# State-space layer: two decoder products of each batch computed in the next batch's turn, and the second norm's affine placed ahead of the first norm's sums and logarithms

## The chip, the cores and the metric

The kernel runs on one core of a Trainium2 chip. The metric is the device time of one execution in microseconds (us); the median of the runs is compared. The core has a matrix engine (TensorE, PE in the profile), a vector engine (VectorE, DVE), a scalar engine (ScalarE, ACT), GpSimd (POOL) and SyncE (SP), which here only issues DMAs. Each engine works through its own list of instructions in order and waits on semaphores.

## The reference

The program is a stack of four layers on an input of 8 batches x 384 channels x 1024 tokens, each layer added to its input after a group norm: attention, a state-space layer, depthwise convolutions, and an RWKV layer. The change touches the second one alone. Its reference, cut (x enters group-normalised; LN is a layer norm over the 384 channels with gain and bias):

```python
fx  = LN(u, ln1_g, ln1_b)                      # the first norm
Bu  = einsum('ph,blh->blp', B_bar, fx)         # complex
xs  = scan over tokens of  lam_bar * x + Bu
y   = gelu(2 * real(einsum('hp,blp->blh', Cc, xs)) + D * fx) + fx
fy  = LN(y, ln2_g, ln2_b)                      # the second norm
z1, z2 = split(fy @ W_enc.T, 2)
y   = (z1 * gelu(z2)) @ W_dec.T + fy
x   = x + y
```

## The kernel before

The layer is `s5_layer`. The channels lie on 128 partitions x 3 tiles (CT = 3), the 1024 tokens are worked in two halves of 512 columns. Everything is float32; one matmul of the program is two passes of the array, so that the trace counts twice as many as the code.

The engines' lists are unrolled over the batches in **turns**. In turn i three batches are in flight: batch i ("here") has its second norm, the encoder, the gates and the decoder; batch i+1 ("after") has the B products, the scan and the C products; batch i+2 ("third") has its group norm and its first norm. Turns -3 to -1 fill this pipeline. Turns 0 to 5 hold all three, turn 6 has no third batch, turn 7 only "here". Names of the steps, with the lines of the kernel before:

- `fill_b` (L1462): 8 products of batch i+1 into PSUM, four per half; `turn_in` (L1288 to L1302) on DVE reads them. `sums` (L831) averages over channels for both norms, on tiles that DVE (`add_tiles`, L1358) or POOL (L1149 to L1157, first norm) have added up. The first norm's squares (`squares`, ACT, L842) and POOL's sums lie in the tile `hid`, which later in the turn holds the gated hidden state.
- `inverses` (ACT, L846 and L849) makes 1/sqrt of the variances by a logarithm and an exponential, first for the second norm of batch i and then for the first norm of batch i+2. `scale` (DVE, L853) multiplies by it, and `affine` (ACT, L1190) applies gain and bias. `f_made` tells PE that `y` is normalised.
- `fill_enc` (L1474): 12 products of batch i, two for each (tile, half), 36 matmuls. ACT makes a gelu of the one (`gates`, L1198) and DVE multiplies it by the other into `hid` (`apply_gate`, L1331).
- `fill_dec` (L1485): 6 products from `hid`, 18 matmuls. DVE adds the normalised `y` to the reloaded input `xres` (`add_residual`, L1336), adds the products (L1344) and measures the result (L1348 to L1354), all in `outputs`.
- `scan` (L1306) and `turn_out` (L1325) on DVE, then `fill_c` (L1495), 24 matmuls, and `activations` (L1372 to L1377).

The products share a ring of 4 PSUM banks. The list `ORDER` gives every product its place, its bank is place % 4, and `wait_for_bank` makes PE wait for the reader of the product four places earlier. SP loads `xin` (the input of batch i+3, for the group norm), stores `xres` when all six outputs of a batch are made, and then reloads it with the next batch.

Of the kernel before, what the change touches and what calls it, by code (L numbers as in the profile page):

```python
# [855 lines left out]
def s5_layer(nc, const, x_in, x_out, moments_out, w):  # L856
# [12 lines left out]
    with ExitStack() as ctx:  # L869
# [19 lines left out]
        hid = sb("hid1", [P, CT, T])  # L889
        u = sb("u1", [P, TILES, T])  # L890
# [208 lines left out]

        ORDER = []  # L1100
        for i in range(-1, B):
            if i + 1 < B:
                ORDER += [("b", i + 1, n) for n in range(2 * TILES)]
            if i >= 0:
                ORDER += [("enc", i, n) for n in range(4 * CT)] + [("dec", i, n) for n in range(2 * CT)]
            if i + 1 < B:
                ORDER += [("c", i + 1, n) for n in range(2 * CT)]
# [15 lines left out]
        def _(sp):  # L1123
            for i in range(-3, B):
# [5 lines left out]
                if i >= 0:  # L1130
                    sp.wait_ge(out_made.sem, out_made.at(2 * CT, i))
                    sp.dma_start(x_out[i:i + 1].rearrange("a (p t) n -> p (a t n)", t=CT), xres[:, :, :].rearrange("p t n -> p (t n)")).then_inc(stored, 16)
                    if i + 1 < B:
                        sp.wait_ge(out_measured.sem, out_measured.at(1, i))
                        sp.wait_ge(stored, 16 * (i + 1))
                        sp.dma_start(xres[:, :, :].rearrange("p t n -> p (t n)"), x_in[i + 1:i + 2].rearrange("a (p t) n -> p (a t n)", t=CT)).then_inc(res_loaded, 16)
# [3 lines left out]
        def _(pool):  # L1140

            for i in range(-2, B):
                if batch(i + 2):
                    f = f1[i % 2]
                    for half in range(2):
                        at = hid[:, 0, cols(half)]
# [5 lines left out]
                    for half in range(2):  # L1152
                        at = hid[:, 0, cols(half)]
                        pool.wait_ge(squared1.sem, squared1.at(half + 1, i + 2))
                        pool.tensor_tensor(at, at, hid[:, 1, cols(half)], ALU.add).then_inc(summed_sq1.next(), 1)
                        pool.wait_ge(summed_sq1.sem, summed_sq1.at(2 * half + 1, i + 2))
                        pool.tensor_tensor(at, at, hid[:, 2, cols(half)], ALU.add).then_inc(summed_sq1.next(), 1)  # L1157

        @block.scalar
        def _(act):  # L1160
# [39 lines left out]
            for i in range(-2, B):  # L1200
# [6 lines left out]
                if batch(i + 2):  # L1207
                    squares(norm1, hid, f1[i % 2], centred1, squared1, i + 2)
                if batch(i):
                    inverses(norm2, varied2, inv_made2, i)  # L1210
                if batch(i + 2):
                    inverses(norm1, varied1, inv_made1, i + 2)
                if batch(i):
                    affine(y, rows["ln2_g"], rows["ln2_b"], scaled2, f_made, i)
# [16 lines left out]
        def _(dve):  # L1231
# [106 lines left out]
            def outputs(i):  # L1338
                for n in range(2 * CT + 1):
                    if n < 2 * CT:  # L1340
# [1128 lines left out]
```

## Time and profile before

| | us |
|---|---|
| median of 3 runs | 4383.45 (4381.31 to 4385.81) |
| the profiled execution: its time | 4377.48 |
| its span | 4375.8 |
| PE busy in the span | 3968.0 (91%) |
| DVE busy | 3072.4 (70%) |
| ACT busy | 2265.1 (52%) |
| POOL busy | 1373.9 (31%) |

The state-space layer takes from about 1852 to 2779 us of the span. The shares of busy time are averages over four different layers, and say nothing on this one; what bounds it is read from the list of instructions in order of time (the timeline) of its turns, where the brackets give the idle time of the engine before an instruction and what ended it. Turn 2 runs from 2202 to 2305 us. "us" behind a start is the sum of the durations of the merged instructions; the end of a matmul is modelled. Starts are the better ruler.

### The profile page before, as it was taken

To read this page: it belongs to the slowest core of one execution; us is meant where nothing else is said; L and a number is where in the kernel's file an instruction comes from. 1 tells how busy PE (TensorE), PEld (TensorE's weight loads), DVE (VectorE), ACT (ScalarE), POOL (GpSimd) and SP (SyncE) were. 2 spreads that over 40 slices of the span, in tenths; PEclk is the share of its full clock that TensorE was granted. 3 is DMA by queue.
4 is the path that set the end of the run, shared out by engine and by line. 5 is a ranking of instruction groups with operands and counts; after the bars stand their busy time and mean duration, and the time that the engine had idled before them with its cause. 6 is when DMAs were issued, how large, how long until landed. Compare 5 with 4: busy or idle time off the path is not lost. (4 is left out here: it accounts for less than half of the span.)

```text
span 4375.8 us, 53839 instructions
## 1 busy us (share of the span) xinstructions
PE 3968.0 (91%) x17283; PEld 2342.1 (54%) x17283; DVE 3072.4 (70%) x3124; ACT 2265.1 (52%) x3601; POOL 1373.9 (31%) x1108
## 2 busy tenths in 40 slices
PE   6999999999999999849999998565899999999999
PEld 5777777777767686424444443244344444444444
DVE  4757575767676765476777766444879879878878
ACT  2858586767677777643333332222445544544544
POOL 2858575757576666521111110222000000000000
PEclk8999999999999999969999999788899999999999
DMA  4323232333333332120111100567110110110110
GB/s 134 87 81 106 75 104 80 100 90 96 93 91 99 86 104 68 57 75 15 58 58 44 44 29 29 145 177 227 47 43 0 43 43 0 43 43 0 43 43 14
DMA packets 114250, 307.91 MB, mean 70 GB/s; under 512 B 47634, under 2 KB 49250, under 8 KB 104306
## 3 DMA queue, kind: packets, MB, share of 16 engines
q1 hardware_dynamic: 105522, 272.56, 20.3%
q0 software_dynamic: 7504, 24.80, 2.2%
q10 hardware_dynamic: 1008, 7.67, 0.5%
q8 instruction: 136, 2.23, 0.2%
q14 instruction: 80, 0.66, 0.1%
HBM read 203.12 MB, written 101.30 MB: 70 GB/s over the span
## 5 line engine op out<-in xcount | busy, mean ns | idle before, releaser
L417 POOL TENSOR_TENSOR probs_lo<-probs,probs_hi 128x512 fp32r<-128x512 f32 x848 | 1170.6, 1396 | 633.2 <-ACT probs L463 612.6
L530 DVE TENSOR_REDUCE maxima<-m_psum 128x1 fp32r<-128x1024 f32 x512 | 625.1, 1222 | 364.9 <-PE m_psum L706 364.0
L462 ACT ACTIVATE probs_hi<-s_psum 128x512 fp32r<-128x512 f32 x1024 | 613.2, 599 | 380.2 <-PE o_psum L735 218.6
L2390 PE MATMUL psum<-mixes,last_weights 128*128 128x512 f32 x1728 | 751.1, 592 | 0.0
L463 ACT ACTIVATE probs<-s_psum 128x512 f32<-128x512 f32 x1024 | 609.0, 595 | 0.0
L2390 PEld LDWEIGHTS psum<-mixes,last_weights 128*128 128x128 f32 x1728 | 327.5, 190 | 409.8 <-issue 409.8
L719 PE MATMUL s_psum<-q_all,k_hi 128*128 128x512 f32 x1024 | 429.7, 420 | 25.4 <-ACT probs L463 25.1
L735 PE MATMUL o_psum<-probs_lo,v 128*112 128x512 f32 x1024 | 411.4, 402 | 13.6 <-DVE probs_lo L610 6.5
L720 PE MATMUL s_psum<-q_all,k_lo 128*128 128x512 f32 x1024 | 403.0, 394 | 0.0
L730 PE MATMUL o_psum<-probs_hi,v 128*112 128x512 f32 x1024 | 402.7, 393 | 0.0
L2397 PE MATMUL psum<-xp,last_weights 128*128 128x512 f32 x864 | 383.2, 597 | 18.3 <-DVEq L2274 13.3
L706 PE MATMUL m_psum<-k_hi,q_all 128*128 128x512 f32 x1024 | 342.2, 416 | 31.5 <-DVE maxima L530 18.2
L706 PEld LDWEIGHTS m_psum<-k_hi,q_all 128*128 128x128 f32 x1024 | 289.2, 324 | 73.9 <-DVE maxima L530 26.5
L1474 PE MATMUL psum<-y,enc_w 128*128 128x512 f32 x576 | 263.6, 620 | 30.3 <-ACT y L1190 30.3
L2397 PEld LDWEIGHTS psum<-xp,last_weights 128*128 128x128 f32 x864 | 162.2, 189 | 233.4 <-issue 208.4
L719 PEld LDWEIGHTS s_psum<-q_all,k_hi 128*128 128x128 f32 x1024 | 194.7, 190 | 120.9 <-ACT probs L463 97.3
L1865 PE MATMUL psum<-xt,last_weights 32*32 32x240 f32 (+3 forms) x5376 | 136.6, 453 | 112.5 <-issue 80.1
L735 PEld LDWEIGHTS o_psum<-probs_lo,v 128*112 128x112 f32 x1024 | 178.7, 175 | 89.8 <-POOL probs_lo L417 22.3
L1474 PEld LDWEIGHTS psum<-y,enc_w 128*128 128x128 f32 x576 | 114.2, 200 | 180.3 <-issue 141.7
L610 DVE TENSOR_TENSOR probs_lo<-probs,probs_hi 128x512 fp32r<-128x512 f32 x176 | 193.1, 1097 | 20.1 <-ACT probs L463 18.9
L720 PEld LDWEIGHTS s_psum<-q_all,k_lo 128*128 128x128 f32 x1024 | 193.4, 189 | 25.6
L730 PEld LDWEIGHTS o_psum<-probs_hi,v 128*112 128x112 f32 x1024 | 178.9, 175 | 45.6
(327 smaller groups left out, 6018.8 us busy)
## 6 DMA issues: line engine op xcount, KB each, us to landing
xin<-x SPq DMA_DIRECT2D x17, 1536.0 KB, 6.8
xin<-in_x SPq DMA_DIRECT2D x16, 1536.0 KB, 7.4
k_hi<-k_rows_hi SPq DMA_DIRECT2D x128, 192.0 KB, 3.4
xres<-x SPq DMA_DIRECT2D x16, 1536.0 KB, 7.0
k_rows_hi<-stage_hi SPq DMA_DIRECT2D x48, 256.0 KB, 2.1
k_rows_lo<-stage_lo SPq DMA_DIRECT2D x48, 256.0 KB, 2.3
q_rows_hi<-stage_hi SPq DMA_DIRECT2D x48, 256.0 KB, 2.5
q_rows_lo<-stage_lo SPq DMA_DIRECT2D x48, 256.0 KB, 2.6
```

Source lines behind the costliest of these rows:

```text
L417: pool.tensor_tensor(probs_lo[:, u % RING, :], probs[:, u % RING, :], as_f32(probs_hi[:, u % RING, :]), ALU.subtract).then_inc(pool_low.ne ...
L462: nc.scalar.activation(probs_hi[:, u % RING, :], s_psum[:, u % 2, :], ACT.Exp, scale=SCALE)
L463: nc.scalar.activation(probs[:, u % RING, :], s_psum[:, u % 2, :], ACT.Exp, scale=SCALE).then_inc(exped.next(), 1)
L530: nc.vector.tensor_reduce(maxima[:, g % 2, tile:tile + 1], source, AX.X, ALU.max, negate=True).then_inc(rows_max.next(), 1)
L706: ins = nc.tensor.matmul(pair_of(other)[:, half, :], q_all[:, g % SLOTS, tile::KEYS], k_hi[:, g % SLOTS, cols_of(half)], start=True, stop= ...
L719: nc.tensor.matmul(s_psum[:, u % 2, :], k_hi[:, h % SLOTS, keys], q, start=True, stop=False)
L720: nc.tensor.matmul(s_psum[:, u % 2, :], k_lo[:, h % SLOTS, keys], q, start=False, stop=True).then_inc(scored.next(), 1)
L730: nc.tensor.matmul(o_psum[0:USED, half, :], v[:, tile, h, :], probs_hi[:, u % RING, :], start=(tile == 0), stop=False)
L735: nc.tensor.matmul(o_psum[0:USED, half, :], v[:, tile, h, :], probs_lo[:, u % RING, :], start=False, stop=(tile == KEYS - 1)).then_inc(wei ...
L1474: ins = nc.tensor.matmul(bank("enc", i, 2 * n + k), enc_w[:, t, first + m * P:first + (m + 1) * P], y[:, t, cols(half)], start=(t == 0), s ...
L2390: ins = nc.tensor.matmul(bank, conv_w[:, t, down, factor, m * P:(m + 1) * P], mixes[:, factor, t, down:down + S, :].rearrange("p a b -> p ...
L2397: ins = nc.tensor.matmul(bank.rearrange("p (a b) -> p a b", b=S), weights[:, t, m * P:(m + 1) * P], rows_of(t, half), start=(t == 0), stop ...
```

## The change

It does five things.

1. `fill_dec` and `outputs` take a range. Of a batch's six decoder products, n = 0 to 3 are computed in its own turn and n = 4 and 5 in the next one, by PE behind `fill_b` and ahead of the first norm's second `sums`; DVE adds and measures them behind `turn_in`. The last batch computes all six in its own turn. `ORDER` follows.
2. POOL's sums and ACT's squares of the first norm move from `hid` into a tile of their own, `first_sums`, since `hid` now holds data of the batch before at that time.
3. On ACT, `affine` of the second norm stands ahead of `inverses` of the first norm.
4. On DVE, `scale` of the first norm moves behind `moments` and the first `scan`, and two scans stand behind it.
5. SP stores batch i-1 and reloads `xres` for batch i in turn i instead of at the end of turn i-1.

```diff
+        first_sums = sb("first_sums", [P, CT, T])
...
+        EARLY = 4
+        def early(i):
+            return EARLY if i + 1 < B else 2 * CT
         for i in range(-1, B):
             if i + 1 < B:
                 ORDER += [("b", i + 1, n) for n in range(2 * TILES)]
+            if i >= 1:
+                ORDER += [("dec", i - 1, n) for n in range(EARLY, 2 * CT)]
             if i >= 0:
-                ORDER += [("enc", i, n) for n in range(4 * CT)] + [("dec", i, n) for n in range(2 * CT)]
+                ORDER += [("enc", i, n) for n in range(4 * CT)] + [("dec", i, n) for n in range(early(i))]
@@ block.sync, behind the load of xin
-                if i >= 0:
-                    sp.wait_ge(out_made.sem, out_made.at(2 * CT, i))
-                    sp.dma_start(x_out[i:i + 1].rearrange("a (p t) n -> p (a t n)", t=CT), xres[:, :, :].rearrange("p t n -> p (t n)")).then_inc(stored, 16)
-                    if i + 1 < B:
-                        sp.wait_ge(out_measured.sem, out_measured.at(1, i))
-                        sp.wait_ge(stored, 16 * (i + 1))
-                        sp.dma_start(xres[:, :, :].rearrange("p t n -> p (t n)"), x_in[i + 1:i + 2].rearrange("a (p t) n -> p (a t n)", t=CT)).then_inc(res_loaded, 16)
+                if i >= 1:
+                    store(i - 1)
+                    sp.wait_ge(out_measured.sem, out_measured.at(1, i - 1))
+                    sp.wait_ge(stored, 16 * i)
+                    sp.dma_start(xres[:, :, :].rearrange("p t n -> p (t n)"), x_in[i:i + 1].rearrange("a (p t) n -> p (a t n)", t=CT)).then_inc(res_loaded, 16)
+            store(B - 1)
@@ block.scalar
                 if batch(i):
                     inverses(norm2, varied2, inv_made2, i)
+                    affine(y, rows["ln2_g"], rows["ln2_b"], scaled2, f_made, i)
                 if batch(i + 2):
                     inverses(norm1, varied1, inv_made1, i + 2)
                 if batch(i):
-                    affine(y, rows["ln2_g"], rows["ln2_b"], scaled2, f_made, i)
                     gates(i, 0, 2)
@@ block.vector
-                if third:
-                    scale(norm1, f1[i % 2], inv_made1, scaled1, i + 2)
+                if batch(i - 1):
+                    outputs(i - 1, EARLY, 2 * CT)
                 if batch(i + 3):
                     moments(i + 3)
                 if after:
                     scan(i + 1, 0)
-                    scan(i + 1, 1)
+                if third:
+                    scale(norm1, f1[i % 2], inv_made1, scaled1, i + 2)
                 if here:
                     apply_gate(i, 0)
                 if after:
+                    scan(i + 1, 1)
                     scan(i + 1, 2)
...
-                    outputs(i)
+                    outputs(i, 0, early(i))
@@ block.tensor
                 if after:
                     fill_b(i + 1, 1, 2, TILES)
+                if batch(i - 1):
+                    fill_dec(i - 1, EARLY, 2 * CT)
                 if third:
-                    sums(norm1, norm_psums[0], hid[:, 0, :], summed_sq1, varied1, i + 2)
+                    sums(norm1, norm_psums[0], first_sums[:, 0, :], summed_sq1, varied1, i + 2)
                 if here:
                     fill_enc(i)
-                    fill_dec(i)
+                    fill_dec(i, 0, early(i))
```

PE in turn 2, before (matmuls as the code counts them; f_1 is the normalised batch i+1, `norm_1` belongs to the second norm, `norm_0` to the first):

```order
L1462 MATMUL psum<-f_1,b_w 128x512 x6
L831 MATMUL norm_1<-z,col_mean 128x512 x2
L1462 MATMUL psum<-f_1,b_w 128x512 x9
L831 MATMUL norm_0<-hid,col_mean 128x512 x2
L1462 MATMUL psum<-f_1,b_w 128x512 x3
L831 MATMUL norm_1<-z,col_mean 128x512 x2
L1462 MATMUL psum<-f_1,b_w 128x512 x6
L831 MATMUL norm_0<-hid,col_mean 128x512 x2
L1474 MATMUL psum<-y,enc_w 128x512 x36
L1485 MATMUL psum<-hid,dec_w 128x512 x18
L1495 MATMUL psum<-u,c_w 128x512 x24
```

and now, where L1479, L1491, L1502 and L1512 are the new lines of the b, enc, dec and c products:

```order
L1479 MATMUL psum<-f_1,b_w 128x512 x6
L831 MATMUL norm_1<-z,col_mean 128x512 x2
L1479 MATMUL psum<-f_1,b_w 128x512 x9
L831 MATMUL norm_0<-first_sums,col_mean 128x512 x2
L1479 MATMUL psum<-f_1,b_w 128x512 x3
L831 MATMUL norm_1<-z,col_mean 128x512 x2
L1479 MATMUL psum<-f_1,b_w 128x512 x6
L1502 MATMUL psum<-hid,dec_w 128x512 x6
L831 MATMUL norm_0<-first_sums,col_mean 128x512 x2
L1491 MATMUL psum<-y,enc_w 128x512 x36
L1502 MATMUL psum<-hid,dec_w 128x512 x12
L1512 MATMUL psum<-u,c_w 128x512 x24
```

Six matmuls on `hid` (the two products put off by turn 1) stand between the last b products and the first norm's sums of squares, and twelve instead of eighteen stand behind the encoder.

DVE in turn 2 from the end of `turn_in` to the first two gates, before:

```order
L1302 TENSOR_TENSOR u<-u,prod 128x512
L853 TENSOR_TENSOR f_0<-f_0,ln_inv 128x3x512 x2
L104 BN_STATS gn_stats<-xin 128x6 x6
L115 BN_AGGR gn_both<-gn_stats 128x2
L118 SCALAR_TENSOR_TENSOR gn_both<-gn_both 128x1
L1306 SCALAR_TENSOR_TENSOR z<-decay,u 128x1024 x2
L1331 TENSOR_TENSOR hid<-gate,psum 128x512
L1306 SCALAR_TENSOR_TENSOR z<-decay,u 128x1024
L1331 TENSOR_TENSOR hid<-gate,psum 128x512
```

and now, where L1315 is the end of `turn_in`, L1357 to L1369 are `outputs`, L1319 is the scan and L1344 the gate:

```order
L1315 TENSOR_TENSOR u<-u,prod 128x512
L1357 TENSOR_TENSOR xres<-xres,psum 128x512 x2
L1361 BN_STATS out_stats<-xres 128x6 x2
L1367 BN_AGGR x_moments<-out_stats 128x2
L1369 SCALAR_TENSOR_TENSOR x_moments<-x_moments 128x1
L104 BN_STATS gn_stats<-xin 128x6 x6
L115 BN_AGGR gn_both<-gn_stats 128x2
L118 SCALAR_TENSOR_TENSOR gn_both<-gn_both 128x1
L1319 SCALAR_TENSOR_TENSOR z<-decay,u 128x1024
L853 TENSOR_TENSOR f_0<-f_0,ln_inv 128x3x512 x2
L1344 TENSOR_TENSOR hid<-gate,psum 128x512
L1319 SCALAR_TENSOR_TENSOR z<-decay,u 128x1024 x2
```

Six instructions of `outputs` (two sums, two measurements, two small ones) stand ahead of the moments, and the first gate has one scan less and these six more in front of it.

ACT in turn 2, from the logarithms of the second norm (`norm_1`) to the gates, before:

```order
L846 ACTIVATE ln_inv<-norm_1,eps 128x512 x2
L849 ACTIVATE ln_inv<-ln_inv 128x512 x2
L846 ACTIVATE ln_inv<-norm_0,eps 128x512 x2
L849 ACTIVATE ln_inv<-ln_inv 128x512 x2
L1190 ACTIVATE y<-y,ln_b_c,ln_g_c 128x512 x6
L1198 ACT_TABLE_LOAD
L1198 ACTIVATE gate<-psum 128x512 x2
```

and now:

```order
L846 ACTIVATE ln_inv<-norm_1,eps 128x512 x2
L849 ACTIVATE ln_inv<-ln_inv 128x512 x2
L1202 ACTIVATE y<-y,ln_b_c,ln_g_c 128x512 x6
L846 ACTIVATE ln_inv<-norm_0,eps 128x512 x2
L849 ACTIVATE ln_inv<-ln_inv 128x512 x2
L1210 ACT_TABLE_LOAD
L1210 ACTIVATE gate<-psum 128x512 x2
```

The six affine instructions on `y` moved ahead of the four instructions of the first norm's (`norm_0`) logarithms and exponentials.

## Rows read from the trace of the kernel before

**Rows 1.** Timeline of PE in turn 2: start, us, engine, line, instruction, count, idle before.

```profile
2202.36 5.40 PE L1462 MATMUL psum<-f,b_w 128*128 128x512 f32 x12
...
2228.42 1.02 PE L831 MATMUL norm<-hid,col_mean 128*128 128x512 f32 x2
2231.05 1.12 PE L831 MATMUL norm<-hid,col_mean 128*128 128x512 f32 x2 [1.61 <-POOL hid L1157]
2236.25 32.87 PE L1474 MATMUL psum<-y,enc_w 128*128 128x512 f32 x72 [4.08 <-ACT y L1190]
2268.96 15.61 PE L1485 MATMUL psum<-hid,dec_w 128*128 128x512 f32 x36
2284.41 20.76 PE L1495 MATMUL psum<-u,c_w 128*128 128x512 f32 x48
...
2305.15 5.40 PE L1462 MATMUL psum<-f,b_w 128*128 128x512 f32 x12
```

**Rows 2.** Timeline of PE in other turns, from turn 0 to turn 7.

```profile
1995.26 5.40 PE L1462 MATMUL psum<-f,b_w 128*128 128x512 f32 x12
...
2544.15 34.22 PE L1474 MATMUL psum<-y,enc_w 128*128 128x512 f32 x72 [4.08 <-ACT y L1190]
...
2614.26 5.31 PE L1462 MATMUL psum<-f,b_w 128*128 128x512 f32 x12
...
2639.02 31.17 PE L1474 MATMUL psum<-y,enc_w 128*128 128x512 f32 x72 [0.34 <-ACT y L1190]
...
2724.47 32.81 PE L1474 MATMUL psum<-y,enc_w 128*128 128x512 f32 x72 [5.49 <-ACT y L1190]
```

**Rows 3.** Stretches: length, busy of each engine, granted TensorE clock, DMA share, GB/s.

```profile
2236.00:2242.00 6.00, 5.75 (x10) 2.54 (x11) 5.92 (x8) 4.19 (x6) 0.00 (x0) 0.69 0.00 0
2614.00:2706.00 92.00, 91.66 (x213) 40.13 (x213) 62.42 (x75) 19.77 (x26) 0.00 (x0) 1.00 0.09 35
```

**Rows 4.** Timeline of ACT in turn 2.

```profile
2232.93 1.15 ACT L849 ACTIVATE ln_inv<-ln_inv 128x512 f32<-128x512 f32 x2
2233.99 4.33 ACT L1190 ACTIVATE y<-y,ln_b_c,ln_g_c 128x512 f32<-128x512 f32 x6
```

**Rows 5.** Timeline of DVE in turn 2, from the second norm's scale to the fourth gate.

```profile
2227.39 5.22 DVE L853 TENSOR_TENSOR y<-y,ln_inv 128x1536 f32<-128x1536 f32 x2 [0.26 <-ACT ln_inv L849]
...
2234.94 3.41 DVE L853 TENSOR_TENSOR f<-f,ln_inv 128x1536 f32<-128x1536 f32 x2
2238.27 3.64 DVE L104 BATCH_NORM_STATS2 gn_stats<-xin 128x6 f32<-128x512 f32 x6
...
2242.55 4.47 DVE L1306 TENSOR_TENSOR_SCAN z<-decay,u 128x1024 f32<-128x1024 f32 x2
...
2254.83 0.68 DVE L1331 TENSOR_TENSOR hid<-gate,psum 128x512 f32<-128x512 f32 x1
...
2259.98 0.68 DVE L1331 TENSOR_TENSOR hid<-gate,psum 128x512 f32<-128x512 f32 x1
```

**Rows 6.** Timeline of DVE in turn 2, end of the outputs.

```profile
2284.68 0.69 DVE L1344 TENSOR_TENSOR xres<-xres,psum 128x512 f32<-128x512 f32 x1 [1.28 <-PE psum L1485]
...
2287.06 0.22 DVE L1354 SCALAR_TENSOR_TENSOR x_moments<-x_moments 128x1 f32<-128x1 f32 x1
```

**Rows 7.** DMA issues of turn 2: count, KB each, median us from issue to landing.

```profile
x<-xres SPq DMA_DIRECT2D x1, 1536.0 KB, 5.0
xres<-x SPq DMA_DIRECT2D x1, 1536.0 KB, 6.2
```

**Rows 8.** Timeline of PE in turn -1, while the pipeline fills.

```profile
1935.73 1.88 PE L831 MATMUL norm<-hid,col_mean 128*128 128x512 f32 x4
```

**Rows 9.** Timeline of POOL in turn -1.

```profile
1932.83 1.27 POOL L1151 TENSOR_TENSOR hid<-hid,f 128x512 f32<-128x512 f32 x1
```

**Rows 10.** Timeline of DVE in turns -2 and -1.

```profile
1915.05 3.65 DVE L104 BATCH_NORM_STATS2 gn_stats<-xin 128x6 f32<-128x512 f32 x6
...
1948.47 3.43 DVE L853 TENSOR_TENSOR f<-f,ln_inv 128x1536 f32<-128x1536 f32 x2 [0.61 <-ACT ln_inv L849]
```

More of the change, by code:

```diff
@@ L1123, in _, with store @@
         def _(sp):
+            def store(i):
+                sp.wait_ge(out_made.sem, out_made.at(2 * CT, i))
+                sp.dma_start(x_out[i:i + 1].rearrange("a (p t) n -> p (a t n)", t=CT), xres[:, :, :].rearrange("p t n -> p (t n)")).then_inc(stored, 16)
             for i in range(-3, B):
@@ L1145, in _ @@
                     for half in range(2):
-                        at = hid[:, 0, cols(half)]
+                        at = first_sums[:, 0, cols(half)]
                         if half == 0:
@@ L1152, in _ @@
                     for half in range(2):
-                        at = hid[:, 0, cols(half)]
+                        at = first_sums[:, 0, cols(half)]
                         pool.wait_ge(squared1.sem, squared1.at(half + 1, i + 2))
-                        pool.tensor_tensor(at, at, hid[:, 1, cols(half)], ALU.add).then_inc(summed_sq1.next(), 1)
+                        pool.tensor_tensor(at, at, first_sums[:, 1, cols(half)], ALU.add).then_inc(summed_sq1.next(), 1)
                         pool.wait_ge(summed_sq1.sem, summed_sq1.at(2 * half + 1, i + 2))
-                        pool.tensor_tensor(at, at, hid[:, 2, cols(half)], ALU.add).then_inc(summed_sq1.next(), 1)
+                        pool.tensor_tensor(at, at, first_sums[:, 2, cols(half)], ALU.add).then_inc(summed_sq1.next(), 1)
         @block.scalar
@@ L1207, in _ @@
                 if batch(i + 2):
-                    squares(norm1, hid, f1[i % 2], centred1, squared1, i + 2)
+                    squares(norm1, first_sums, f1[i % 2], centred1, squared1, i + 2)
                 if batch(i):
                     inverses(norm2, varied2, inv_made2, i)
+                    affine(y, rows["ln2_g"], rows["ln2_b"], scaled2, f_made, i)
                 if batch(i + 2):
@@ L1336, in add_residual, with outputs @@
                 nc.vector.tensor_tensor(xres[:, :, cols(half)], xres[:, :, cols(half)], y[:, :, cols(half)], ALU.add).then_inc(res_added.next(), 1)
-            def outputs(i):
-                for n in range(2 * CT + 1):
-                    if n < 2 * CT:
+            def outputs(i, first, end):
+                for n in range(first, end + 1):
+                    if n < end:
                         m, half = n % CT, n // CT
@@ L1344, in outputs @@
                         nc.vector.tensor_tensor(xres[:, m, cols(half)], xres[:, m, cols(half)], bank("dec", i, n), ALU.add).then_inc(out_made.next(), 1)
-                    if n > 0:
+                    if n > first:
                         last = n - 1
@@ L1348, in outputs @@
                         nc.vector.bn_stats(out_stats[:, last, :], xres[:, last % CT, cols(last // CT)]).then_inc(step.next(), 1)
+                if end < 2 * CT:
+                    return
                 out = moments_out[:, i, :]
@@ L1476, in fill_enc, with fill_dec @@
                         ins.then_inc(hidden.next(), 1)
-            def fill_dec(i):
-                for n in range(2 * CT):
+            def fill_dec(i, first, end):
+                for n in range(first, end):
                     m, half = n % CT, n // CT
-                    if m == 0:
+                    if m == 0 or n == first:
                         pe.wait_ge(hid_made.sem, hid_made.at(CT * (half + 1), i))
@@ L1515, in _ @@
                 if third:
-                    sums(norm1, norm_psums[0], hid[:, 0, :], summed_x1, averaged1, i + 2)
+                    sums(norm1, norm_psums[0], first_sums[:, 0, :], summed_x1, averaged1, i + 2)
                 if after:
```

## The prediction, written before the changed kernel was run

> **What bounds the kernel now.** I read the timeline of each engine over one turn of the state-space layer, PE first. Turn 2 takes 102.79 us from its first b product to the next turn's [rows 1]. In it PE does 220 passes of the array. The 48 c passes take 20.6 us from start to start, 0.43 us each, and the 36 dec passes 15.45 us, the same [rows 1]; so PE's work is 94.4 us, and it waits or runs slowly for the other 8.4. All of that lies at one place. PE sits idle 1.61 us for POOL's sums of squares, then 4.08 us for ACT's affine of `y` [rows 1]. The 72 encoder passes that follow take 32.71 us from start to start, and 31.0 in turn 6 (31.17 less the 0.16 by which a duration there exceeds the distance of starts) [rows 1, 2]. The difference is the clock: 0.69 of 2.4 GHz was granted just behind the waits, that is, part of the stretch ran at 1.2 GHz, while all of turn 6, where PE idles 0.34 us, had 1.00 [rows 2, 3]. It costs 1.7 us in turn 2 and 3.05 in turn 5 [rows 1, 2]. The other 0.4 us are spread. So PE bounds every turn, but for one hole of some 8 us.
>
> The affine of `y` begins at 2233.99 with no idle before it, behind the exponentials of the first norm (2232.93), which in turn waited for POOL and PE [rows 4]. Its own input was ready much earlier: DVE scales `y` from 2227.39 on, two instructions in 5.22 us, so the first half is there by 2230.9 at the latest (5.22 less one unhindered 1.71) [rows 5]. The second norm thus waits for the first for no reason of data.
>
> **The new front of a turn (turns 1 to 5).** I keep turn 2's clock times. Up to 2228.42 PE has the same list [rows 1]. Then come 12 passes of the two put-off products (12 x 0.43 = 5.15), which cover POOL's end at about 2231, and 4 passes of sums (1.72): the encoder can start at 2235.3, 32.9 us into the turn, if what it waits for is there.
> - Affine: first half of `y` at 2230.9, three instructions of 0.72 (4.33 / 6) [rows 4]: 2233.0. In time. Before, this came at 2236.25.
> - Banks: the two products take banks whose readers are `turn_in`'s first four instructions of the second half, done before 2227.39 [rows 5]. The first encoder product takes that of the third b product, read right behind the scale of `y` (2232.6 + 0.6 = 2233.2). In time. The third and fourth encoder products wait for the put-off outputs on DVE, made by 2236.2, needed from 2240.5. In time.
> - The first norm is pushed back: sums by 2235.3, logarithms and exponentials (4 ACT instructions, 2.5 us) by 2238, the first gelu about 2239. DVE wants that norm's inverse only at 2244.6 (below).
>
> **The gates on DVE.** This is where the new order costs something. `turn_in` ends at 2234.94 [rows 5]. Then stand the outputs: one sum, two measurements and two small ones take 2.6 us (2284.68 to 2287.28) [rows 6], another sum 0.6: 3.2. Moments 4.28 (2238.27 to 2242.55), one scan 2.2 (4.47 / 2), the first norm's scale 3.33 (2234.94 to 2238.27) [rows 5]: 2248.0, and the first gate is done about 2248.65. PE's sixth encoder product needs it, five products of 2.58 behind 2235.3, at 2248.2. So PE waits about 0.45 us. From below it could be 0; from above, the outputs now cost as much as in their old place, where they come at PE's pace of 2.57 each, 5.1, and the wait is 2.4. I take 0.45, since both products are finished (2233.6) before DVE asks. Further gates lose nothing: DVE's step from gate to gate is 5.15 (2254.83 to 2259.98) [rows 5], and PE's pair of products takes 5.16. There is no cover left, though: here DVE and PE run neck and neck.
>
> **The turn sums.** Encoder 31.0 at full clock, four dec products 15.45 x 4 / 6 = 10.3, c products 20.6, group matmul 0.15.
> - Turns 1 to 4: 32.9 + 31.0 + 0.45 + 10.3 + 20.6 + 0.15 = 95.4 each, 381.6.
> - Turn 5 has no moments ahead of its gates and no group matmul behind: 94.8.
> - Turn 0 has nothing put off to it. The encoder starts with the affine at 2233.0, 30.6 into the turn: 92.7. It keeps 2.4 us of idle time; if the clock falls for it, up to 3 more.
>
> Together 569.1. Before, these six turns took 2614.26 - 1995.26 = 619.0 [rows 2]. **Gain 49.9.**
> - Turn 6 has the same number of products; its 0.34 us wait [rows 2] goes: gain 0.3.
> - Turn 7 has two products more. They stand where PE idles 5.49 us before the encoder [rows 2]: 5.15 us at full clock, 10.3 at half. The encoder's 32.81 there holds 1.6 of slow clock [rows 2], which busy PE may get back. Between a gain of 1.6 and a loss of 3.2; I take a gain of 1.0, because PE already runs its last sums just before.
> - Start: in turn -2 the moments (4.28) now stand ahead of the first norm's scale [rows 10]. That delay goes through ACT to POOL, whose sums for batch 1 end at 1938.4 and not 1934.1 [rows 9]. PE wants the second half at 1936.6 [rows 8]: 1.8 late. DVE's 0.61 us wait before the scale of turn -1 [rows 10] goes, as the moments fill it. A loss of 1.2; bounds 0 and 4.3.
>
> Sum: 49.9 + 0.3 + 1.0 - 1.2 = 50.0. The profiled execution's 4377.48 becomes 4327.5; it lay 6 us under the median, whose turns are the same, so I take the gain off the median: 4383.45 - 50.0 = **4333**.
>
> What lies beside: the DMAs. SP issues the store at 2236.2 instead of behind the outputs of the turn before, and the reload behind it: 5.0 and 6.2 us to land [rows 7], so `xres` is there at 2247.5. DVE adds it behind the fourth gate, about 2263.7. POOL's list is the same; its own tile removes no wait that showed.
>
> **Rivals.**
> - *DVE becomes the bound at the gates.* By the upper bound above, 2 us more in each of turns 1 to 4, 8 in all: 4341. For it: no slack. Against it: all six instructions have their inputs.
> - *The slow clock stays.* Turns 0 to 5 lose 1.7 to 3.05 us each as before [rows 1, 2], about 2.2 on average, 13 in all, though the idle time is down to some 0.5 us: 4346. Against it: turn 6 ran at 1.00 throughout with 0.34 us idle [rows 3]. The Trainium skill, "TensorE: Matmul & The Clock Gate", section "A second HAM failure mode: psum-queue depth-cycling", says that short idles between groups of matmuls that cycle through PSUM banks can be enough to make the clock swing; this kernel has such a ring of four banks, and by that rule this rival would hold, at its 4346. The trace disagrees in turn 6.
> - *The change does not do what it says:* the put-off products cannot start until `turn_in` is through (2234.94), because the ring holds them. Then the encoder starts at 2241.8, and turns 1 to 5 take 101.5 plus the slow clock, as before; only turn 0's 11 us are left: 4372. Against it: the banks' readers are done by 2227.39.
> - *The reload of `xres` comes late.* It is now inside the turn that needs it. It decides from about 2267, where the fifth gate, queued behind the add on DVE, holds a bank that PE wants; each us later costs one in 7 turns. To end 0.2% slower it must land 28 us after the 2247.5 of the rows, and gives 4392 there. Against it: 11.2 us for both transfers [rows 7] and a DMA queue with nothing else in it.
>
> **How the numbers follow.** The forecast 0.75, with a range of its own of 4326 (no wait at the gates, no loss at the start, the clock back in turn 7) to 4339 (turn 0's clock, a wait of 1 us, the loss in turn 7). DVE at the gates 0.10, slow clock 0.06, the ring 0.03, the late reload 0.06, of which half ends within 0.2%. The range 4325 to 4346 takes in the first three. A measurement of this kernel can tell about 0.2% from no change: faster by more 0.94, within it 0.03, slower 0.03.
>
> **What would show it.** Right: turns 1 to 4 at 95 to 96 us from first b product to first b product; no idle over 1 us before the encoder; clock 1.00 in turns 1 to 6; the encoder at 31.0 to 31.5; L853 on `f` behind a scan; PE waiting at most once a turn, in the encoder, for `hid` by DVE. Wrong: an idle of 2 us or more inside the encoder (DVE), encoder stretches above 32.5 with no idle inside (clock), an idle before the put-off products (ring), or DVE idle before L1349 for a DMA (reload). Turn 0's first b product more than 3 us later than 1995.26 [rows 2] would show that the start was mis-sized.

## The result, and the profile after

| | before | after |
|---|---|---|
| median | 4382.38 us (4379.58 to 4385.81, 4 runs) | 4331.14 us (4326.31 to 4335.67, 4 runs) |
| ratio, 95% interval | | 0.9883 (0.9865 to 0.99) |
| span of the profiled execution | 4375.8 us | 4329.4 us |
| PE busy in the span | 3968.0 us | 3959.5 us |

The kernel is 51.2 us faster; 50.0 had been forecast, and a time of 4333. To compare the layer alone, I measure from one event that both kernels have: the end of DVE's last instruction that builds the scan's tables, at 1911.7 us of the span before and 1917.5 after. From there to the first matmul of the next layer it is 867.7 us before and 817.1 after, 50.6 less. The profiled after entered the layer 5.8 us later, through the attention layer ahead of it, which the change does not touch; that is why the two profiled executions lie only 46 us apart.

First the timeline of PE in turn 2 after: start, summed duration, engine, line, instruction, count, idle before and what ended it. It answers to [rows 1].

```profile
2190.27 5.40 PE L1479 MATMUL psum<-f,b_w 128*128 128x512 f32 x12
...
2216.32 5.31 PE L1502 MATMUL psum<-hid,dec_w 128*128 128x512 f32 x12
2221.47 1.88 PE L831 MATMUL norm<-first_sums,col_mean 128*128 128x512 f32 x4
2223.19 13.04 PE L1491 MATMUL psum<-y,enc_w 128*128 128x512 f32 x30
2236.53 18.29 PE L1491 MATMUL psum<-y,enc_w 128*128 128x512 f32 x42 [0.30 <-DVE hid L1344]
2254.65 10.46 PE L1502 MATMUL psum<-hid,dec_w 128*128 128x512 f32 x24
2264.95 20.76 PE L1512 MATMUL psum<-u,c_w 128*128 128x512 f32 x48
...
2285.69 5.40 PE L1479 MATMUL psum<-f,b_w 128*128 128x512 f32 x12
```

Both waits of [rows 1], 1.61 us for POOL and 4.08 us for ACT, are gone. Twelve passes of the put-off products stand in their place, and one new wait of 0.30 us appears, for DVE's first gate. The turn takes 95.42 us instead of 102.79.

The stretches of PE's clock come next, with the columns of [rows 3]: turns 1 to 5 as a whole, turn 6, the front of turn 7, and its encoder.

```profile
2094.00:2571.00 477.00, 475.88 (x1113) 209.57 (x1112) 374.14 (x448) 165.29 (x215) 61.52 (x40) 1.00 0.12 47
...
2571.00:2662.00 91.00, 91.00 (x212) 40.02 (x212) 62.40 (x75) 19.77 (x26) 0.00 (x0) 1.00 0.09 35
2662.00:2681.00 19.00, 12.59 (x22) 4.60 (x20) 13.96 (x16) 9.51 (x11) 0.00 (x0) 0.73 0.00 0
2681.00:2712.00 31.00, 31.00 (x74) 13.79 (x73) 9.31 (x13) 7.10 (x11) 0.00 (x0) 1.00 0.25 102
```

The first number behind the length is PE's busy time, and the third from the end is the granted clock. In turns 1 to 5 PE is busy for 475.88 of 477 us, at the full 2.4 GHz, where the stretch behind the waits of turn 2 had had 0.69 before [rows 3], and those of the other turns 0.50 to 0.76.

The third view is DVE's timeline from the end of `turn_in` to the second gate, in the same turn (compare [rows 5]; four lines of small instructions are left out):

```profile
2222.28 0.68 DVE L1315 TENSOR_TENSOR u<-u,prod 128x512 f32<-128x512 f32 x1
2222.88 1.27 DVE L1357 TENSOR_TENSOR xres<-xres,psum 128x512 f32<-128x512 f32 x2
2224.07 1.27 DVE L1361 BATCH_NORM_STATS2 out_stats<-xres 128x6 f32<-128x512 f32 x2
...
2225.98 3.65 DVE L104 BATCH_NORM_STATS2 gn_stats<-xin 128x6 f32<-128x512 f32 x6
...
2230.27 2.28 DVE L1319 TENSOR_TENSOR_SCAN z<-decay,u 128x1024 f32<-128x1024 f32 x1
2232.47 3.40 DVE L853 TENSOR_TENSOR f<-f,ln_inv 128x1536 f32<-128x1536 f32 x2
2235.79 0.68 DVE L1344 TENSOR_TENSOR hid<-gate,psum 128x512 f32<-128x512 f32 x1
2236.39 4.47 DVE L1319 TENSOR_TENSOR_SCAN z<-decay,u 128x1024 f32<-128x1024 f32 x2
2240.77 0.66 DVE L1344 TENSOR_TENSOR hid<-gate,psum 128x512 f32<-128x512 f32 x1
```

No bracket stands anywhere, in the lines left out either: DVE finds every input there and works without a gap, and its first gate still ends (2236.4) just behind the moment when PE wants the bank (2236.2). DVE is full there, and PE but for its 0.30 us, as the prediction said.

All kernels of this study stand in one table. Every column is a distance between events of one profile: "start" runs from the end of the last table instruction to turn 0's first b product, a turn from its first b product to the next turn's, turn 7 to the next layer's first matmul. "Layer" is the sum. Each line is one profile; the start of one and the same kernel differed by 1.6 us between two of them, and differences of a few microseconds in the last column are no surer than that.

| kernel | start | turn 0 | turns 1 to 4, each | turn 5 | turn 6 | turn 7 | layer |
|---|---|---|---|---|---|---|---|
| before | 83.6 | 103.9 | 102.5 to 103.2 | 104.0 | 91.8 | 73.3 | 867.7 |
| after | 85.1 | 92.3 | 95.4 | 94.7 | 91.2 | 72.1 | 817.1 |
| after, again | 86.7 | 92.3 | 95.4 | 94.7 | 91.2 | 72.1 | 818.6 |
| affine alone | 82.4 | 104.3 | 103.0 to 104.4 | 97.0 | 91.8 | 73.2 | 862.3 |
| put-off alone | 86.8 | 98.7 | 100.6 to 102.2 | 100.5 | 91.2 | 71.2 | 854.4 |
| nothing put off | 86.7 | 97.4 | 97.4 | 98.6 | 91.8 | 74.7 | 839.0 |
| old vector order | 82.9 | 99.2 | 99.3 | 94.7 | 91.2 | 71.4 | 836.6 |
| one put off | 84.9 | 94.9 | 96.9 | 94.7 | 91.2 | 73.1 | 826.5 |
| three put off | 86.6 | 89.7 | 94.9 | 94.7 | 91.2 | 73.3 | 815.0 |
| wait for the first norm | 86.4 | 99.1 | 98.8 | 96.9 | 91.2 | 71.3 | 840.1 |
| five reloads | 86.9 | 92.3 | 103.2 to 105.3 | 103.2 | 101.6 | 80.7 | 881.8 |
| moments late | 81.6 | 91.9 | 94.9 | 94.7 | 91.2 | 72.0 | 810.9 |

### The profile page after: what moved, and what is told of

Its sections match the earlier page's. It is cut to its first block and busy times, and to the rows that moved or that the text cites. A ratio compares the mean times of both kernels' runs of the same rounds, so it can differ in the third digit from the quotient of the medians.

```text
span 4329.4 us, 53846 instructions
## 1 busy us (share of the span) xinstructions
PE 3959.5 (91%) x17283; PEld 2344.6 (54%) x17283; DVE 3069.7 (71%) x3124; ACT 2266.7 (52%) x3601; POOL 1374.8 (32%) x1108
## 5 line engine op out<-in xcount | busy, mean ns | idle before, releaser
L2416 PE MATMUL psum<-xp,last_weights 128*128 128x512 f32 x864 | 382.0, 596 | 18.3 <-DVEq L2293 13.3
L1491 PE MATMUL psum<-y,enc_w 128*128 128x512 f32 x576 | 249.9, 593 | 1.3 <-DVE hid L1344 1.1
L1512 PE MATMUL psum<-u,c_w 128*128 128x512 f32 x384 | 168.6, 599 | 24.3 <-DVE u L1338 24.3
```

The lines of the kernel that those rows point to most:

```text
L1491: ins = nc.tensor.matmul(bank("enc", i, 2 * n + k), enc_w[:, t, first + m * P:first + (m + 1) * P], y[:, t, cols(half)], start=(t == 0), s ...
L2416: ins = nc.tensor.matmul(bank.rearrange("p (a b) -> p a b", b=S), weights[:, t, m * P:(m + 1) * P], rows_of(t, half), start=(t == 0), stop ...
```

## Experiments: which part brings it

By the theory the change has three parts that move time: ACT's affine ahead of the first norm's logarithms, two products put off, and a new order on DVE. Each of them closes the hole of 8 us a turn only in part, and the wait moves to the next latest input when one part is missing.

**Affine alone** (`e1_affine_alone`). The kernel before with only this edit:

```diff
                 if batch(i):
                     inverses(norm2, varied2, inv_made2, i)
+                    affine(y, rows["ln2_g"], rows["ln2_b"], scaled2, f_made, i)
                 if batch(i + 2):
                     inverses(norm1, varied1, inv_made1, i + 2)
                 if batch(i):
-                    affine(y, rows["ln2_g"], rows["ln2_b"], scaled2, f_made, i)
```

> Only the affine of the second norm is moved ahead of the first norm's logarithms, in the kernel before; nothing is put off and DVE keeps its old order. Theory (DVE and PE are neck and neck at the gates): the encoder starts some 3.9 us earlier, at 29.8 us into the turn, but the first gate does not come earlier, it even comes 2 us later, since DVE's scale of the first norm, which stands ahead of it, now waits for that norm's later inverse. PE waits about 4.6 us inside the encoder for the first gate. Turns of 101.5 to 103 us against 102.8, total 4372 to 4382. Rival (PE's front alone sets the turn): turns of 97.5, total about 4351.

Measured: 4378.43 us against 4380.78, ratio 0.9998 (0.9989 to 1.0008), no difference that the runs can tell. Timeline of PE, turn 2:

```profile
2232.05 1.13 PE L831 MATMUL norm<-hid,col_mean 128*128 128x512 f32 x2 [1.60 <-POOL hid L1157]
2233.18 13.14 PE L1474 MATMUL psum<-y,enc_w 128*128 128x512 f32 x30
2250.44 19.89 PE L1474 MATMUL psum<-y,enc_w 128*128 128x512 f32 x42 [4.11 <-DVE hid L1331]
```

The encoder starts without the 4.08 us wait, and five products later PE waits 4.11 us for DVE's first gate. The clock falls there too (0.66 in the next 5 us). DVE shows why the gate is late, in its timeline of the same turn:

```profile
2237.71 3.43 DVE L853 TENSOR_TENSOR f<-f,ln_inv 128x1536 f32<-128x1536 f32 x2 [1.70 <-ACT ln_inv L849]
2241.05 3.65 DVE L104 BATCH_NORM_STATS2 gn_stats<-xin 128x6 f32<-128x512 f32 x6
...
2245.34 4.47 DVE L1306 TENSOR_TENSOR_SCAN z<-decay,u 128x1024 f32<-128x1024 f32 x2
2249.72 0.66 DVE L1331 TENSOR_TENSOR hid<-gate,psum 128x512 f32<-128x512 f32 x1
```

Ahead of the gate stand the scale of the first norm, which now itself waits 1.70 us for its later inverse, the moments and two scans. Only turn 5, which has no moments, gets shorter: 97.0 instead of 104.0 us.

**Put-off alone** (`e2_putoff_alone`). The kernel after with the affine moved back behind the first norm's inverses, the reverse of the diff above.

> All of the change but the affine, which stays behind the first norm's logarithms. Theory: the put-off products push those logarithms back, and with them the affine, so that PE still idles 4.2 us in one piece ahead of the encoder and the clock falls there: turns 1 to 5 about 101.5 us, turn 0 98.8, total 4366 to 4374. Rival (each part brings its own share, the put-off products simply fill the old hole): encoder start unchanged at 33.9 us into the turn, turns of 97.6, total about 4350.

Measured: 4367.30 us, ratio 0.9971 (0.9961 to 0.998). The timeline of PE in turn 2:

```profile
2234.08 1.88 PE L831 MATMUL norm<-first_sums,col_mean 128*128 128x512 f32 x4
2240.03 32.56 PE L1491 MATMUL psum<-y,enc_w 128*128 128x512 f32 x72 [4.07 <-ACT y L1202]
```

The put-off products cover POOL's 1.6 us, but push the first norm's sums back, and the affine behind them with it: the wait for ACT stays at 4.07 us and the encoder at slow clock. Of the 50.6 us, 13.3 are left.

**Affine and DVE order, nothing put off** (`e9_nothing_put_off`). The kernel after with

```diff
-        EARLY = 4
+        EARLY = 2 * CT
```

and the two places where products are put off skipped.

> The whole change with all six products in their own turn: affine ahead, the new order on DVE, the store and reload late, nothing put off. Theory: encoder at 29.8 us into the turn, first gate 3.1 us earlier than in the changed kernel, a wait of about 0.3 in the encoder, PE idle 1.6 for POOL and the clock held: turns 0 to 5 at 97.6, total 4350 (33 of the 50 us without the put-off products). Rival (the clock falls for a 1.6 us idle followed by a short one): turns of 99 to 100, total 4360 to 4365.

Measured: 4351.14 us, ratio 0.9928 (0.9912 to 0.9945). Of the gain 28.7 us remain. What stays is the wait of 1.61 to 1.63 us for POOL in each of turns 0 to 5, with an encoder of 31.6 us behind it instead of 31.06, and in turn 5 a fall of the clock (below). PE in turn 2:

```profile
2229.29 1.12 PE L831 MATMUL norm<-first_sums,col_mean 128*128 128x512 f32 x2 [1.63 <-POOL first_sums L1169]
2230.42 31.58 PE L1491 MATMUL psum<-y,enc_w 128*128 128x512 f32 x72
```

This kernel also settles a rival. It has the tile `first_sums` and the later store and reload (points 2 and 5 of the change), and PE's wait for POOL still ends 28.7 us into the turn, as in the kernel before (2231.05 less 2202.36 [rows 1]). So these two points bring nothing of their own at that place.

**Old order on DVE** (`e3_old_vector_order`). The kernel after with

```diff
+                if third:
+                    scale(norm1, f1[i % 2], inv_made1, scaled1, i + 2)
                 if batch(i + 3):
                     moments(i + 3)
                 if after:
                     scan(i + 1, 0)
-                if third:
-                    scale(norm1, f1[i % 2], inv_made1, scaled1, i + 2)
+                    scan(i + 1, 1)
                 if here:
                     apply_gate(i, 0)
                 if after:
-                    scan(i + 1, 1)
```

> The changed kernel with DVE's old order: scale of the first norm, moments, two scans, then the first gate. Theory: the first gate 2.2 us later, so a wait of 2.5 us inside the encoder in turns 1 to 4 (turns of 97.6 against 95.4), 4.5 in turn 0 (96.8), none in turn 5, and the start 1.6 us shorter: total about 4343. Rival (DVE has slack, the order on it costs nothing): turns of 95.4, total 4330.

Measured: 4347.54 us, ratio 0.9922 (0.9906 to 0.9939). PE's timeline of turn 2, and then the 5 us from just ahead of the wait's end, with the granted clock as the third number from the end:

```profile
2229.99 13.04 PE L1491 MATMUL psum<-y,enc_w 128*128 128x512 f32 x30
2245.48 19.99 PE L1491 MATMUL psum<-y,enc_w 128*128 128x512 f32 x42 [2.45 <-DVE hid L1344]
```

```profile
2245.00:2250.00 5.00, 4.52 (x7) 1.98 (x8) 5.00 (x5) 0.60 (x1) 0.00 (x0) 0.66 0.00 0
```

The wait is 2.43 to 2.46 us in turns 1 to 4. But the 42 passes take 19.99 instead of 18.29 us: the clock fell for some microseconds and cost another 1.7. A wait of 2.15 us more thus costs 3.9 us a turn. I had counted the wait alone.

The four runs together: affine alone leaves 5.4 us of the layer's gain, put-off alone 13.3 (with the new DVE order in it), affine and DVE order 28.7, affine and put-off without the DVE order 31.1, all three 50.6. No part can be credited with a share of its own, and neither the put-off products nor the DVE order was run quite alone. Each takes away one of three waits (POOL's sums, ACT's affine, DVE's first gate) that end within a few microseconds of each other.

## Experiments: how many products to put off

**One** (`e4_putoff_one`) and **three** (`e5_putoff_three`): the kernel after with `EARLY = 5` and `EARLY = 3`.

> The changed kernel with one decoder product put off and not two. Theory: the encoder starts at 30.4 us into the turn and not 32.9, but the first gate on DVE comes only 1.2 us earlier (one sum and one measurement less ahead of it), so the wait in the encoder grows from 0.3 to 1.75 us: turns 1 to 4 of 96.8 against 95.4, turn 5 95.1, turn 0 94.9; total about 4340. Rival (PE's hole of 1.6 us is all that has to be filled, one product of 2.6 us does it): turns of 95.4, total 4333.

Measured: 4339.30 us, ratio 0.9914 (0.9885 to 0.9943), two runs; turns 1 to 4 at 96.90 us.

> Three products put off. Theory: the encoder starts 35.5 us into the turn, behind the first gate's slack: no wait in it, turns 1 to 4 of 94.95 against 95.4, turn 0 89.7, and turn 7 2.6 us longer, since the third product no longer fits its hole: total 4329 to 4331. Rival (DVE, with a third sum and measurement ahead of the gates, becomes the bound): turns of 96 and more, total 4334 or more.

Measured: 4328.69 us, ratio 0.989 (0.9861 to 0.9919), two runs; turns 1 to 4 at 94.87 us, turn 0 at 89.7. The total can't be told from that of two products put off; the turns can. The first gate on DVE fixes the end of a turn's front: with one product, PE comes to it earlier and waits 1.77 us; with two it waits 0.30; with three it no longer waits, and only PE's own work is left. A third product is worth 0.54 us in each of turns 1 to 4 and 2.6 us in turn 0, and costs 1.2 in turn 7, where I had expected 2.6. The steps are those of one sum: five encoder products against DVE's chain.

## Experiments: the rivals

**The clock** (`e6_wait_for_first_norm`). To see what a wait of about 2 us ahead of the encoder costs, PE waits there for the first norm's inverse, which it does not need:

```diff
                 if here:
+                    if third:
+                        pe.wait_ge(inv_made1.sem, inv_made1.at(2, i + 2))
                     fill_enc(i)
```

> The changed kernel with one more wait: PE starts the encoder only when the first norm's inverses are made, which makes an idle of 2.1 us in one piece in turns 1 to 5 and of some 5 us in turn 0. It asks what an idle does to the clock. Theory: 2.1 us don't lower it (1.6 did not): turns 1 to 4 of 97.2 (2.1 more, less the 0.3 of the wait inside the encoder), encoder at 31.0; turn 0 falls to 1.2 GHz for some us; total about 4347. Rival (the clock falls as it did behind 1.6 + 4.1 us): encoder at 32.4 to 34, turns of 99, total 4355 to 4360.

Measured: 4353.81 us, ratio 0.9938 (0.9918 to 0.9958). First the PE lines of turns 1 and 5, then the 5 us behind both waits:

```profile
2139.21 32.86 PE L1491 MATMUL psum<-y,enc_w 128*128 128x512 f32 x72 [1.96 <-ACT ln_inv L849]
...
2534.36 31.17 PE L1491 MATMUL psum<-y,enc_w 128*128 128x512 f32 x72 [1.96 <-ACT ln_inv L849]
```

```profile
2139.00:2144.00 5.00, 4.79 (x7) 2.03 (x8) 4.65 (x10) 1.65 (x3) 0.00 (x0) 0.66 0.66 280
2534.00:2539.00 5.00, 4.64 (x11) 2.20 (x12) 4.82 (x6) 2.19 (x3) 0.00 (x0) 1.00 0.74 315
```

In turns 1 to 4 the clock fell behind a wait of 1.96 us (0.66 in the stretch of turn 1, the encoder at 32.86 us in all four), and in turn 5 it did not behind a wait of the same length (1.00, 31.17 us). My expectation that 2 us would leave the clock alone was wrong in four turns of five. With turn 0, where the wait is 5.08 us and the encoder takes 33.36, the edit costs 21.5 us of the layer against the repetition of after.

The other kernels add to this. Between turn 0 and turn 6 of all twelve, single waits of PE of 1.60 to 1.63 us, with no second one in the 10 us behind them, come 19 times, and the clock fell behind one of them: turn 5 of "nothing put off", with an encoder of 32.86 us where the five turns before had 31.57 or 31.58 behind the same wait. "One put off" has four waits of 1.77 us, and it fell behind none. Behind every wait of 2.4 us and more in these turns it fell, behind those of 0.34 and less never. So between 1.6 and 2 us the length alone does not decide; what else enters is left open.

**A late reload** (`e7_five_reloads`). SP loads `xres` five times, one behind the other, with the same data, and DVE waits for the fifth:

```diff
-                    sp.dma_start(xres[...], x_in[i:i + 1]...).then_inc(res_loaded, 16)
+                    for again in range(5):
+                        if again:
+                            sp.wait_ge(res_loaded, 16 * (5 * i - 4 + again))
+                        sp.dma_start(xres[...], x_in[i:i + 1]...).then_inc(res_loaded, 16)
...
-                dve.wait_ge(res_loaded, 16 * (i + 1))
+                dve.wait_ge(res_loaded, 16 * (5 * i + 1))
```

> The changed kernel with the reload of xres done five times over, one after the other, with the same data, so that it lands some 27 us later in each of turns 1 to 7. Theory (the prediction's rival with its place and price): DVE waits 11 to 12 us at the add behind the fourth gate, PE waits for the fifth gate's bank about 8.5 us at the second decoder product of each turn, 60 us in all: about 4391, at 28 us late the point of no gain. Rival (the reload has more slack, or the delay is taken up elsewhere in the turn): under 4370.

Measured: 4394.66 us, ratio 1.0036 (1.0021 to 1.0052). DVE's and then PE's timeline in turn 2:

```profile
2272.78 1.76 DVE L1352 TENSOR_TENSOR xres<-xres,y 128x1536 f32<-128x1536 f32 x1 [10.01 <-DMA xres<-x]
```

```profile
2275.19 10.66 PE L1505 MATMUL psum<-hid,dec_w 128*128 128x512 f32 x18 [6.74 <-DVE hid L1347]
```

The mechanism of the rival is real: DVE idles 10.01 us for the load, the fifth gate is queued behind it, and PE waits 6.74 us inside the decoder and then runs slowly (18 passes in 10.5 us from start to start instead of 7.7). In all, PE's waits for the fifth gate come to 46.9 us in turns 1 to 7 (5.61 to 7.89 each, where 8.5 had been expected), and the layer is 63.2 us longer than in the repetition of after, so that some 16 us are left. The passes behind the waits, which run slowly in every one of these turns (18 in 9.45 to 10.66 us instead of 7.89), make up 15 of them. The sum came near the 60 expected because a shorter wait and an unpriced clock made up for each other. In the kernel after the reload has no grip. Its DMA issues in turn 2, microseconds to landing in the last column:

```profile
x<-xres SPq DMA_DIRECT2D x1, 1536.0 KB, 5.0
xres<-x SPq DMA_DIRECT2D x1, 1536.0 KB, 6.5
```

SP issues the reload at 2229.24, so it lands at 2235.7, and DVE asks for it at 2251.6: 16 us of slack.

## Experiments: the same kernel again, and a better one

**After, again** (`a0_after`).

> The changed kernel again, as the measure for the next one on the same chip: about 4331, turns 1 to 4 of 95.4 us.

Measured: 4334.07 us against 4379.20, ratio 0.9891 (0.9874 to 0.9907). All turns repeat within 0.1 us; the start is 1.6 us longer.

**Moments late** (`e8_moments_late`). The moments of the group norm are needed only behind the turn's c products. They go from their place ahead of the first gate to behind the last gate, and in turn -2 the first norm's scale goes back ahead of them:

```diff
-                if batch(i + 3):
+                if i < 0 and third and not after:
+                    scale(norm1, f1[i % 2], inv_made1, scaled1, i + 2)
+                if i < 0 and batch(i + 3):
                     moments(i + 3)
                 if after:
                     scan(i + 1, 0)
-                if third:
+                if third and after:
                     scale(norm1, f1[i % 2], inv_made1, scaled1, i + 2)
...
                     apply_gate(i, 5)
+                    if batch(i + 3):
+                        moments(i + 3)
                     outputs(i, 0, early(i))
```

> The changed kernel with DVE's moments of the group norm moved from ahead of the first gate to behind the sixth, where DVE waits for the decoder, and with the first norm's scale ahead of the moments again in turn -2. Theory: the first gate comes 4.3 us earlier, the 0.3 us wait in the encoder goes (turns 1 to 4 of 95.1), and the start is 1.6 us shorter: 2.8 us less than the changed kernel, about 4328, which the total can hardly tell and the turns can. Rival (the moments at the new place delay the outputs and with them the banks of the c products): turns above 95.4, no gain.

Measured: 4325.08 us (4319.11 to 4328.4), ratio 0.987 (0.9853 to 0.9886), the lowest median of all. PE's timeline of turn 2:

```profile
2214.58 1.88 PE L831 MATMUL norm<-first_sums,col_mean 128*128 128x512 f32 x4
2216.30 31.06 PE L1495 MATMUL psum<-y,enc_w 128*128 128x512 f32 x72
2247.20 10.46 PE L1506 MATMUL psum<-hid,dec_w 128*128 128x512 f32 x24
2257.50 20.76 PE L1516 MATMUL psum<-u,c_w 128*128 128x512 f32 x48
```

No wait is left in the turn. Its 94.87 us are PE's work: 220 passes of 0.43 and a small rest. In the layer it is 6.2 us ahead of after and 7.7 ahead of its repetition. About 2.6 of that are in turns 0 to 4, where 1.2 had been expected (turns of 95.1), and the larger part, 3.6 to 5.1, is in the start, which had been put at less than half of it. The intervals of this kernel and of after overlap, so the difference between these two rests on the profiles.

## Why the prediction was right

By its own steps:

- **The encoder start at 32.9 us.** Measured 32.92 (2223.19 less 2190.27 in turn 2). The put-off products stand right behind the b products with no wait for a bank; the rival in which the ring holds them is out.
- **The affine in time.** ACT has the first three instructions done 29.8 us into the turn (below), 3 us before the encoder wants them, 30.6 having been forecast. The prediction took only the first half as needed at that point; the second half is done at 2222.8, also in time, but by 0.4 us only. The timeline of ACT:

```profile
2217.84 2.22 ACT L1202 ACTIVATE y<-y,ln_b_c,ln_g_c 128x512 f32<-128x512 f32 x3 [2.06 <-DVE y L853]
2220.59 2.23 ACT L1202 ACTIVATE y<-y,ln_b_c,ln_g_c 128x512 f32<-128x512 f32 x3 [0.53 <-DVE y L853]
2222.72 1.35 ACT L846 ACTIVATE ln_inv<-norm,eps 128x512 f32<-128x512 f32 x2
```

- **DVE's chain to the first gate.** Forecast 3.2 for the outputs, 4.28, 2.2 and 3.33; measured 3.10, 4.29, 2.20 and 3.32. The gate ends 46.1 us into the turn, forecast 46.3, and PE's wait is 0.26 to 0.30 instead of 0.45. Taking the outputs at DVE's own speed, and not at PE's pace, was the choice that mattered, and it held: their inputs were ready.
- **The turns.** Forecast 92.7, four of 95.4, and 94.8; measured 92.29, four of 95.4, and 94.73. The six turns took 568.7 us, 569.1 forecast. In turn 0 two small errors offset each other: the encoder started at 29.8 us and not 30.6, and took 31.4 from start to start and not 31.0. The turn kept 1.63 us of idle time, 2.4 forecast, and its clock stayed at 1.00.
- **The clock.** Forecast to come back, and it did: 1.00 in turns 0 to 6. The Trainium skill, "TensorE: Matmul & The Clock Gate", section "A second HAM failure mode: psum-queue depth-cycling", has short idles between groups of matmuls that cycle through banks make the clock swing. The traces do not bear it out for the 0.26 to 0.30 us of the kernel after, which cycles through the same four banks; between turn 0 and turn 6 they show the clock fall only behind waits of 1.6 us and more.
- **Turn 6 and turn 7.** Gains of 0.6 and 1.2 us, 0.3 and 1.0 forecast. In turn 7 the put-off products took 5.9 us of the hole, partly at slow clock, and the encoder behind them got the full clock: 31.06 instead of 32.81 [rows 2]. Timeline of PE in turn 7 after:

```profile
2671.90 3.78 PE L831 MATMUL norm<-z,col_mean 128*128 128x512 f32 x4 [3.17 <-DVE z L1375]
2675.48 6.10 PE L1502 MATMUL psum<-hid,dec_w 128*128 128x512 f32 x12
2681.41 31.06 PE L1491 MATMUL psum<-y,enc_w 128*128 128x512 f32 x72
```

- **The start: the one term that was mis-sized.** Forecast a loss of 1.2 us, bounds 0 and 4.3. The pair of profiles before and after gives 1.5, but all profiles together give more. The four kernels with the old DVE order in turn -2 (before, affine alone, old vector order, moments late) have starts of 81.6 to 83.6, mean 82.6; the eight with the new one 84.9 to 86.9, mean 86.3. That is 3.6 us. The pair shows less because before's first 30 b products were the slowest of its four kernels (15.98 us, the others 14.87 to 15.54). The delay has the place that was named: PE waits for POOL's sums, 1.90 us after, 1.8 forecast. What was left out shows in the repetition of after:

```profile
1944.77 2.07 PE L831 MATMUL norm<-first_sums,col_mean 128*128 128x512 f32 x2 [2.20 <-POOL first_sums L1163]
1946.63 8.68 PE L1479 MATMUL psum<-f,b_w 128*128 128x512 f32 x18
```

Behind the wait the two sums take 2.07 us instead of 1.13 and the 18 b passes 8.68 instead of 7.89 (both in after's first profile): 1.7 us of slow clock. The prediction priced the wait, and not the clock that a wait can bring with it. This slow clock shows in six of the eight kernels with the new order; in after's first profile and in "one put off" it does not, and their starts are the shortest, 85.1 and 84.9. It is the same omission as in the expectation of "old vector order". The prediction's own sign, turn 0's first b product more than 3 us later than 1995.26, was no good measure: it came at 2002.58, but 5.8 of these 7.3 us lie ahead of the layer. With 3.6 in place of 1.2 the sum would have been 47.6 plus the 0.9 by which turns 0 to 7 beat it: 48.5, and a time of 4335, still in the range. That the forecast lay within 2 us of the median is in part luck, since repetitions of one kernel spread over 7 to 9 us.

- **The rivals.** DVE as the bound: it is one, by 0.3 us a turn, and it becomes a real one as soon as its order is the old one. The late reload: real as a mechanism, 16 us away. Its price was too low: in "five reloads" the data landed some 26 us later in turn 2, for which the prediction's one microsecond for each in 7 turns gives about 45, and the layer grew by 63.

- **Sums of the prediction that don't come out.** Of the 8.4 us that PE loses in turn 2 before, 1.61, 4.08 and 1.7 leave 1.0 and not 0.4. And the slow clock cost not 1.7 to 3.05 us in turns 0 to 5 but 1.4 to 3.05 (encoders of 32.57 us in turn 4 to 34.22 in turn 5, against 31.17). Neither enters the forecast.

One thing the prediction did not see: it treated the new DVE order as a cost at the gates. The run with the old order shows it to be a part of the gain in its own right, without which 19.5 us of the layer's 50.6 are lost.

## What to carry to other kernels

Where several inputs of a bound engine's next step arrive within a few microseconds of each other, write down the arrival of each, engine by engine, in the new order; the gain of an edit is the distance to the next latest, and parts that each gain little may gain much together. Price a wait of a couple of microseconds on PE with its clock: in this layer a fall of the clock behind it cost another 1.3 to 3 us. When an order is changed for the steady turns, go through the turns that fill the pipeline too, since there the same edit can cost what it gains elsewhere.

## What the hardware showed that was not expected

- The clock can fall behind an idle time of 1.62 us and stay up behind one of 1.96 us. Neither the kernel nor the place decides: each of the two kernels ("nothing put off" and "wait for the first norm") has both outcomes behind the same wait at the same place of the turn. A fall cost from 1.3 us (encoder 32.86 against 31.57) to 3.05 us (34.22 in turn 5 of before against 31.17 in turn 6 [rows 2]).
- DVE and POOL slow each other where POOL and a DVE instruction with both inputs in SBUF run together. The timeline of POOL and of DVE after, in turn -1:

```profile
1939.90 1.59 POOL L1163 TENSOR_TENSOR first_sums<-first_sums,f 128x512 f32<-128x512 f32 x1
1941.46 1.71 POOL L1161 TENSOR_TENSOR first_sums<-f 128x512 f32<-128x512 f32 x1
```

```profile
1938.87 0.68 DVE L1311 TENSOR_TENSOR prod<-psum,tables 128x512 f32<-128x512 f32 x1
...
1940.29 1.75 DVE L1315 TENSOR_TENSOR u<-u,prod 128x512 f32<-128x512 f32 x1
```

The second DVE instruction takes 1.75 us here and 0.68 in turn 2, where POOL is idle; POOL's take 1.59 and 1.71 instead of 1.27. The first one reads one of its inputs from PSUM and keeps its 0.68 us, though POOL works beside it then too. The Trainium skill, "SBUF — State Buffer", section "Who interferes with whom", says that a DVE instruction with two SBUF inputs contends with a GpSimd instruction that reads SBUF, and that the lock on the shared ports is exclusive. The trace agrees: the DVE instruction ends at 1942.04, 0.55 us behind the end of POOL's first one, not far from its own length when alone, as if it had begun only there. It bears on this kernel's waits: in turn 2 after, POOL's last two sums take 1.72 and 2.67 us beside DVE's scale of `y`, 1.85 more than alone, and the wait of PE for POOL that the change hides was 1.61. That the one makes the other is an argument; no run moved the two apart.
